# Summing four scan states with four identity products in the last quarter of each direction of a Mamba layer

## The reference, cut to what matters

```python
_, h = jax.lax.associative_scan(comb, (dA, dBx), axis=1)
y = jnp.einsum('blds,bls->bld', h, Cm) + D * xs
y = y * jax.nn.silu(z)
return y @ W_out
```

## Time and profile before

| what | value |
|---|---|
| time, median of 3 runs (lowest, highest) | 7561.89 us (7559.71, 7574.29) |
| the profiled execution: its time, its span | 7566.64 us, 7564.8 us |
| DVE busy | 6668.0 us, 88% |
| PE busy (matmul records) | 6573.8 us, 87% |
| ACT busy | 6172.1 us, 82% |
| PE loads of the stationary operand | 3737.1 us, 49% |
| POOL busy | 886.3 us, 12% |
| mean granted clock of PE | 0.951 of full speed |

### The profile page before, as it was taken

The page is one execution under the profiler, slowest core; times in us unless marked ns, Lnnn a source line. Parts: engine busy times, 40 slices in busy tenths (PEclk is TensorE's granted clock), DMA queues, the critical chain, the costliest instruction groups (busy, mean ns, idle before and its releaser), DMA issues. The chain is left out here.

```text
span 7564.8 us, 112453 instructions
## 1 busy us (share of the span) xinstructions
PE 6573.8 (87%) x33290; PEld 3737.1 (49%) x33290; DVE 6668.0 (88%) x8110; ACT 6172.1 (82%) x13680; POOL 886.3 (12%) x555
## 2 busy tenths in 40 slices
PE   6888887889999999999999999999999999998570
PEld 3444444445555555555555555555555555554240
DVE  2788888989999999999999999999999999999743
ACT  5777777778888888888988889888898888988334
POOL 0053545430000000000000000000000000000085
PEclk9999898999999999999999999999999999999775
DMA  3243333333343333333334333343333333333366
GB/s 106 109 139 133 129 130 107 124 119 138 140 147 131 143 138 140 147 132 142 140 138 147 126 148 142 137 147 134 140 146 136 143 133 140 147 136 134 132 123 215
DMA packets 282207, 1035.92 MB, mean 137 GB/s; under 512 B 37570, under 2 KB 129526, under 8 KB 273824
## 3 DMA queue, kind: packets, MB, share of 16 engines
q1 hardware_dynamic: 248352, 1014.00, 36.8%
q0 software_dynamic: 33792, 21.18, 1.8%
HBM read 955.77 MB, written 90.98 MB: 138 GB/s over the span
## 5 line engine op out<-in xcount | busy, mean ns | idle before, releaser
L878 DVE TENSOR_TENSOR_SCAN hs<-dA,hs 128x1584 f32<-128x1584 f32 x512 | 1766.6, 3451 | 1.0 <-ACT dA L689 0.8
L612 ACT ACTIVATE P<-psS,least_s 99x197 f32<-99x197 f32 x4096 | 1488.1, 470 | 228.6 <-DVE least_s L817 226.1
L1079 PE MATMUL psS<-KM,Q 128*99 128x394 f32 x4096 | 1558.6, 504 | 9.0 <-ACT PTs L620 4.2
L689 ACT ACTIVATE dA<-dt_,aneg 128x394 f32<-128x394 f32 x2048 | 1239.2, 642 | 208.3 <-DVE hs L878 190.7
L817 DVE TENSOR_REDUCE least_s<-psS 99x2 f32<-99x394 f32 x2048 | 1076.9, 560 | 120.2 <-PE psS L1079 103.6
L1086 PEld LDWEIGHTS psS<-cst,P 99*99 99x99 f32 x8192 | 851.9, 167 | 495.1 <-ACT P L612 425.0
L1086 PE MATMUL psS<-cst,P 99*99 99x99 f32 x8192 | 988.0, 257 | 93.1 <-ACT P L612 81.5
L620 ACT ACTIVATE PTs<-psS 99x396 f32<-99x396 f32 x2048 | 982.3, 551 | 46.2 <-PE psS L1086 35.1
L869 DVE TENSOR_TENSOR hs<-hs,u 128x1584 f32<-128x1584 f32 x512 | 923.9, 1804 | 95.1 <-DMA hs<-bc_scratch 91.8
L883 DVE TENSOR_TENSOR hs<-hs,cr 128x1584 f32<-128x1584 f32 x512 | 922.6, 1802 | 9.0
L1079 PEld LDWEIGHTS psS<-KM,Q 128*99 128x99 f32 x4096 | 600.2, 165 | 522.6 <-issue 324.4
(11 more groups left out here) (215 smaller groups left out, 9273.5 us busy)
## 6 DMA issues: line engine op xcount, KB each, us to landing
hs<-bc_scratch SPq DMA_DIRECT2D x512, 792.0 KB, 5.4
cr<-bc_scratch SPq DMA_DIRECT2D x512, 792.0 KB, 6.0
pat<-patches SPq DMA_DIRECT2D x64, 1176.0 KB, 8.4
more_scratch<-zeros SPq DMA_DIRECT2D x64, 197.0 KB, 3.2
rows_scratch<-hs SPq DMA_DIRECT2D x1, 12352.0 KB, 42.8
PTs<-more_scratch SPq DMA_DIRECT2D x24, 512.0 KB, 5.6
sum_scratch<-HW SPq DMA_DIRECT2D x64, 148.5 KB
hs<-rows_scratch SPq DMA_DIRECT2D x24, 386.0 KB, 3.3
```

The source lines that it names most:

```text
L612: last = nc.scalar.activation(P[:, r, b, m, 0:T], psS[0:CT, 2 * r + b, m * T:(m + 1) * T], ACT.Exp, bias=least_s[:, r, b, m:m + 1], scale= ...
L689: last = nc.scalar.activation(shifted(dA[:, g % 2, k, :]), images(dt_[:, d, :]), ACT.Exp, scale=aneg[:, d, n:n + 1])
L878: nc.vector.tensor_tensor_scan(h, a, h, 0.0, ALU.mult, ALU.add).then_inc(scan_ready, 1)
L1079: mm(psS[0:CT, 2 * r + b, 0:2 * T].rearrange("p (e t) -> p e t", e=2), Q[:, r, b, q * CT:(q + 1) * CT], KM[:, r, h % 2 * 2:h % 2 * 2 + 2, ...
```

## The change

The addition `half` is no longer done for quarters 3 and 7. For these two, PE's `sum` waits for `output` itself (`out_done`) and adds all four states with four products instead of two. The entries of `half 3` and `half 7` are taken out of DVE's list; the other entries, and the lists of all other engines, stay in their order. The count of `half_summed` that `sum` waits for is adapted to six a step.

```diff
 ORDER = {
     "dve": [
-        ... (3, 'b', 'input', 4), (2, 'f', 'sig', 1), (3, 'b', 'half', 3),
+        ... (3, 'b', 'input', 4), (2, 'f', 'sig', 1),
...
-        (1, 'f', 'score', 1, 3, 0), (3, 'b', 'output', 7), (0, 'f', 'score', 0, 3, 1), (3, 'b', 'half', 7), (0, 'f', 'score', 0, 3, 0), (2, 'b', 'input', 0),
+        (1, 'f', 'score', 1, 3, 0), (3, 'b', 'output', 7), (0, 'f', 'score', 0, 3, 1), (0, 'f', 'score', 0, 3, 0), (2, 'b', 'input', 0),
...
             def half(i, g):
                 dve.wait_ge(out_done, i * QUARTERS + g + 1)
+                assert g % HALF < HALF - 1
...
             def sum_(i, g):
...
-                pe.wait_ge(half_summed, i * QUARTERS + g + 1)
-                for k in range(2):
+                if q == HALF - 1:
+                    pe.wait_ge(out_done, i * QUARTERS + g + 1)
+                else:
+                    pe.wait_ge(half_summed, i * 2 * (HALF - 1) + d * (HALF - 1) + q + 1)
+                for k in range(4 if q == HALF - 1 else 2):
                     last = mm(psY[:, 0:SW], c("ident"), hs[:, g % HBUF, k, :], start=q == 0 and k == 0, stop=False)
                 last.then_inc(acc_done, 1)
```

## The result

The changed kernel takes 7690.91 us (median of 4 runs, 7677.55 to 7704.23), the kernel before 7563.81 (4 runs): a ratio of 1.0164, 95% interval 1.0148 to 1.0180. It is 127 us slower; 133 were forecast, and a time of 7695 us within 7640 to 7730. The profiled execution took 7704.23 us, its span is 7702.4.

What follows compares the result with a forecast made beforehand. A loop through several engines, not one engine, was taken to bound the kernel. Costs of 82.5 us at `sum 7` and 50.6 at `sum 3` sum to 133.1, giving 7695 us, range 7640 to 7730.

Steps and rivals of the forecast that it cites:

- What bounds: Whole step: a loop through several engines sets the end; at quarter 7 it runs `sum 7`, load of B, `input 1`, DVE.
- The additions cost nothing: DVE, quarters 3 and 7: removing `half 3` and `half 7`, 1.78 us a step, gains nothing, as waits cover them.
- `sum 7`: PE, quarter 7: two added products delay the load and `input 1` by 1.33 us a step, 82.5 us over 62 steps.
- `sum 3`: PE, quarter 3: two added products make `up 0` wait 0.74 us in 54 steps and 1.33 in 8, 50.6 us.
- The price of a product: PE, `sum 3` and `sum 7`: two added products cost 1.33 us each time, at 0.33 us a record.
- The clock: PE's granted clock: share of long steps kept at 0.31; none or double would mean 28 us off or on.
- DVE sets the pace: Rival: DVE's own chain sets the end, so removing its additions gains 110 us, giving 7452; chance 0.05.
- Only `sum 7` counts: Rival: the 0.74 us at `up 0` come back in a later wait, 82.5 us remain, giving 7644; chance 0.08.
- PE sets the pace in every step: Rival: all four added products count on PE, 62 x 2.66 = 165 us, giving 7727; chance 0.06.
- Nothing to be seen: Rival: the load issued later could land earlier and the ends cancel, giving near 7562; chance 0.02.

Runs made afterwards that it cites:

- DVE's side alone: The changed kernel with two products in every `sum`, so only DVE's additions of quarters 3 and 7 are gone: 7579.11 us, ratio 1.0001 to the kernel before.
- `ys 1` moved: The kernel before, with `ys 1` placed ahead of `input 1` instead of behind it in DVE's list: 7547.44 us, ratio 0.9962.
- quarter 7 only: The kernel before, with `half 7` taken out and four products in `sum 7`, `half 3` kept: 7634.82 us, ratio 1.0084.
- products behind the release: The kernel before, with two more products in `sum 7`, placed behind `acc_done`, which lets the buffer go: 7605.75 us, ratio 1.0047.
- quarter 3 only: The kernel before, with `half 3` taken out and four products in `sum 3`, `half 7` kept: 7631.01 us, ratio 1.0072.
- skip term early: The changed kernel, with the forward direction's skip term in `sum 2` instead of behind `sum 3`: 7634.52 us, ratio 1.0088 to the kernel before.

## Why the prediction was right

*What bounds.* That the end is set by a loop through DVE, PE, SP and the load, not by DVE, was the step on which the sign hung. The run of DVE's side alone shows that these additions do not set the pace: ratio 1.0001 (0.9990 to 1.0012) with all 128 taken away. That the wait for the load lies on the path is shown by the run with `ys 1` moved. The rule of the Trainium skill that went the other way ("Perfetto Trace Analysis", section "Identifying the Most-Contended Engine": improve the engine of highest occupancy first) pointed to the wrong change here: DVE has the highest occupancy, 88%, and less work on it gave nothing.

*The additions cost nothing.* Right at both places, with the waits named: before `up 1` 1.67 us was forecast and seen; around `scan 0` and the minima the slack shows as 0.19 and 0.40 us. Over the span the waits at lines 869, 878 and 817 grew by 131 us, 2.1 us in each of 62 steps, where about 2.2 were forecast. The fall of DVE's busy time, 100 us, is less than the 125 that were forecast. Those are 128 times the full 0.98 us, but an addition overlaps its neighbour, and 0.89 us from start to start gives 114; the rest is not explained, nor is PE's rise of 148 instead of 170 us.

*`sum 7`.* 1.33 us a step was forecast, the short step grew by 1.40 with quarter 7 only. That the release of the buffer, and with it the load, makes the cost is shown by the run with the products behind the release, 0.41 us in place of 1.40. The prediction saw only this path; the second one, PE's own scores, is hidden behind it.

*`sum 3`.* 0.74 us a step was forecast, the wait at `up 0` is 0.66 us and the short step grew by 0.71. The count of waits at line 835 rose from 74 to 128, to one at each `up`. One term was wrong: the eight steps in which `up 0` already waited were to pay the whole 1.33 us. Before, nine `up 0` waited, 3.2 us in all; after, all 63 that can be told apart wait 0.66 to 0.76 us, 42.5 us in all, and none pays 1.33. So the 50.6 us of the sum were some 39 in this wait, or 62 x 0.71 = 44 in short steps. That the total came within 6 us is in part luck, as 62 x 1.40 = 87 us at `sum 7` is 4 more than its term.

*The price of a product.* 2.66 us for eight records was forecast and seen; the row held. The other price weighed, the rate that the Trainium skill gives in "TensorE: Matmul & The Clock Gate", section "Back-to-back issue gap", had led to an estimate near 7608, 83 us too low: this trace has 0.33 us a record of 396 float32 columns.

*The clock.* The share of long steps was kept as it was, 0.31, and came out at 15 of 49 against 17. That this step was right is partly luck: the other runs have between 1 and 23 long steps, and the bounds of 28 us to either side were needed. The cost itself does not hang on it: the short steps, without a stretch at half clock, grew by 2.01 us.

*The rivals.* "DVE sets the pace" fell with DVE's side alone. "Only `sum 7` counts" fell with quarter 3 only. "PE sets the pace in every step" fell with the products behind the release, and with 0.71 instead of 1.33 us at quarter 3. "Nothing to be seen" fell with the 127 us: the load does not land noticeably earlier when it is issued later (3.99 against 4.05 us from issue to `input 1`, the medians given above).

## What to carry to other kernels

When two engines are each 90% busy, moving work from the busier one to the other need not be a gain: look for what ends each wait at the place of the change, and ask of every instruction that is made longer what its completion releases (here a buffer, and with it a load), not only what stands behind it. An instruction that lies wholly inside a wait can be free to keep and worthless to remove, as the two additions were, and a small independent instruction can be moved into such a wait: that alone gave some 0.3 to 0.4% here. Measure the two sides of a trade apart, and where steps come in two lengths count them before differences of a few tenths of a per cent are read.

## What was not expected

How often a step has a stretch at half clock on PE differs from kernel to kernel: 17 of 49 steps before, 2 with quarter 7 only, 1 with the skip term early, 23 with `ys 1` moved, at 1.5 to 2.1 us each. Each count is of one execution, but the mean granted clock of all runs agrees: 0.949 to 0.953 for the kernel before, 0.952 to 0.956 with quarter 7 only, 0.954 to 0.956 with the skip term early. It hides or adds up to 24 us here (15 long steps at 1.6 us), as much as half of one of the effects looked for. In the step of the kernel before that begins at 4046.28, this is PE's product at which it sets in, and the window of the stretch itself, with the granted clock as the third number from the end:

```profile
4080.79 2.67 PE L1111 MATMUL psS<-O,wts 128*128 128x394 f32 x4 [1.61 <-DVE O L822]
```

```profile
4081.15:4084.56 3.41, 3.41 (x6) 1.69 (x5) 2.44 (x4) 1.58 (x4) 0.00 (x0) 0.50 0.00 0
```

PE had waited 1.61 us for DVE, and the four-record product took 2.67 us instead of the 1.59 of the same product at 4089.18. No run tried to steer it, and what makes it rare in some of these kernels stays open.
